# Flamingo gated block on one core: first loads and TensorE's first products in another order

## The reference, cut to what matters

```
x = x + tanh(g_xattn) * attention(layernorm(x), ctx, ctx, Wq, Wk, Wv)
x = x + tanh(g_ffn) * ffn(layernorm(x), ...)

attention: qh = q Wq^T, kh = k Wk^T, vh = v Wv^T
           scores = causal(qh kh^T / 16); probs = softmax(scores, over the queries)
           out = probs vh
ffn:       xq = quantised(x), gate and up = xq times quantised weights (256 to 704)
           h = quantised(silu(gate) * up); out = h times quantised w_down
```

## Time and profile before

| | |
|---|---|
| time, median of 3 runs | 107.29 us (106.71 to 107.92) |
| the profiled execution's own time | 106.97 us |
| its span | 105.2 us |
| PE / PEld busy | 97.9 us (93%) / 75.0 us (71%) |
| DVE / ACT / POOL busy | 80.6 / 66.1 / 43.4 us |

### The profile page before, as it was taken

How to read it: one execution, slowest core, us unless ns; L and a number is a source line. 1 busy time by engine, 2 the same in 40 slices (tenths; PEclk the granted TensorE clock), 3 DMA queues, 4 the chain that set the end, 5 groups by cost and what they waited for, 6 DMA issues and landing times.

```text
span 105.2 us, 1740 instructions
## 1 busy us (share of the span) xinstructions
PE 97.9 (93%) x564; PEld 75.0 (71%) x564; DVE 80.6 (77%) x211; ACT 66.1 (63%) x125; POOL 43.4 (41%) x78
## 2 busy tenths in 40 slices
PE   7999999999999999999989986999999697899990
PEld 2278888988989898887778973444444386889970
DVE  0544395497999979868597979559999998879991
ACT  0421071657980836639707978789888989799800
POOL 6030345056280835635606595045785560350000
DMA  2999999999305020020754800000000000004555
GB/s 43 329 378 319 393 421 423 411 408 407 119 2 48 0 49 4 18 39 3 148 101 100 161 13 0 0 6 3 0 0 0 0 0 0 0 6 184 215 199 199
DMA packets 11177, 13.54 MB, mean 129 GB/s; under 512 B 6433, under 2 KB 7713, under 8 KB 11169
## 3 DMA queue, kind: packets, MB, share of 16 engines
q1 hardware_dynamic: 10304, 12.39, 36.3%
q10 hardware_dynamic: 864, 1.05, 2.9%
HBM read 10.09 MB, written 2.10 MB: 116 GB/s over the span
## 4 chain that ended last, share of the span: by engine, by line
PE 43%; DVE 26%; DMA 13%; POOL 5%; issue 5%; ACT 4%; ACTq 1%; DVEq 0%; POOLq 0%
PE ps L459 10%; DVE hmax L1087 9%; PE ps L680 9%; PE ps L479 7%; DMA wvT<-in_wvT 5%; PE ps L497 5%; DMA r_wide<-spread 4%; DVE shared L1082 4%; DMA spread<-rstd 4%; PE ps L629 3%; POOL shared L430 2%; DVE bn L916 2%; DVE xs L910 2%; PE ps L685 2%; PE ps L509 2%
## 5 line engine op out<-in xcount | busy, mean ns | idle before, releaser
L629 PE MATMUL ps<-xq,wguT 128*128 128x512 bf16 x80 | 17.4, 379 | 0.8 <-DVE xq L1062 0.8
L430 POOL TENSOR_TENSOR shared<-up_sb,silu 128x1024 f32<-128x1024 f32 x5 | 11.8, 2365 | 9.5 <-ACT up_sb L826 9.5
L629 PEld LDWEIGHTS ps<-xq,wguT 128*128 128x128 bf16 x80 | 7.8, 97 | 10.2 <-issue 1.0
L459 PE MATMUL ps<-wvT,shared 128*128 128x256 f32 x56 | 13.3, 381 | 0.2 <-DMA wvT<-in_wvT 0.2
L479 PE MATMUL ps<-shared,a_sb 128*128 128x256 f32 x56 | 13.3, 380 | 0.0
L1087 DVE TENSOR_REDUCE hmax<-shared 128x1 f32<-128x2048 f32 (+1 forms) x6 | 12.6, 2108 | 0.6 <-POOL shared L430 0.2
L821 ACT ACTIVATE silu<-ps,gu_scale 128x1024 f32<-128x1024 f32 x10 | 11.1, 1113 | 2.3 <-PE ps L629 2.3
L497 PEld LDWEIGHTS ps<-uT,shared 128*128 128x128 f32 x64 | 10.7, 191 | 2.5 <-DVE uT L888 1.3
L497 PE MATMUL ps<-uT,shared 128*128 128x256 f32 (+1 forms) x64 | 12.0, 331 | 0.5 <-DVE uT L888 0.4
L459 PEld LDWEIGHTS ps<-wvT,shared 128*128 128x128 f32 x56 | 10.6, 190 | 2.0 <-DMA shared<-in_xc 0.6
L722 ACT ACTIVATE probs<-neg_scores,neg_max 128x256 f32<-128x256 f32 x8 | 4.1, 508 | 12.4 <-DVE neg_max L896 12.3
(11 more groups left out here) (120 smaller groups left out, 189.0 us busy)
## 6 DMA issues: line engine op xcount, KB each, us to landing
shared<-in_xc SPq DMA_DIRECT2D x6, 512.0 KB, 10.7
out<-xn SPq DMA_DIRECT2D x7, 256.0 KB, 2.0
xs<-in_x SPq DMA_DIRECT2D x3, 512.0 KB, 8.3
shared<-in_wgu SPq DMA_DIRECT2D x3, 512.0 KB, 7.7
wd<-in_wd SPq DMA_DIRECT2D x1, 896.0 KB, 11.7
shared<-in_xc SPq DMA_DIRECT2D x3, 256.0 KB, 6.4
xs<-in_x ACTq DMA_DIRECT2D x2, 256.0 KB, 5.5
r_wide<-spread SPq DMA_DIRECT2D x4, 128.0 KB, 4.5
```

Source lines behind the costliest of these rows:

```text
L430: nc.gpsimd.tensor_tensor(hid[:, 2 * i + 1, :], up_sb[i % 2][:], silu1[i % 2][:], ALU.mult).then_inc(hid_done[1], 1)
L459: last = nc.tensor.matmul(bank2(VB[b])[:, k, :], ctxT(b)[:, e, k * P:(k + 1) * P], weights[:, e, :], start=(e == 0), stop=(e == KT - 1))
L629: last = nc.tensor.matmul(bank(4 * half + 2 * g + c), wguT[:, i, g, k, :], xq[:, k, col:col + CH], start=(k == 0), stop=(k == KT - 1))
```

## The change

The order of the first transfers. Before, the SP queue carried half 0 of Wq, all of Wk, ctxT(0), half 0 of xT(0), xT(1), ctxT(1); the ACT queue half 1 of Wq, x of batch 0, Wv, half 1 of xT(0), x of batch 1, the scalars. After:

- SP: half 0 of Wq, half 0 of Wk, ctxT(0), half 0 of x of batch 0, half 0 of xT(0), ctxT(1), x of batch 1; then the wait ahead of the bulk is for half 1 of xT(0) in place of Wv;
- ACT: half 1 of Wq, half 1 of Wk, Wv, half 1 of x of batch 0, half 1 of xT(0), xT(1), the scalars.

Each half is 128 KB, each whole 256 KB. TensorE runs 9 warming products in place of 10, waits for each half of Wk by itself, does both value tiles of batch 0 ahead of the projection of batch 0, and the first value tile of batch 1 behind that projection. In the first pass of the loop `spread_deviation(1)` stands behind `project_queries(1)` and not ahead of it, and only the second value tile of batch 1 is left there. DVE does the statistics of batch 1 behind `scale_queries(0, ...)` in place of ahead of it.

```
--- before.py
+++ after.py
@@ -42,7 +42,7 @@
 MASKED = -1e30
 SCORE_SCALE = float(D) ** -0.5
 
-WARM_AT_START = 10
+WARM_AT_START = 9
 WARM_BEFORE_MAX = 2
 WARM_AT_BARRIER2 = 7
 FIRST_SLOTS = 6
@@ -191,7 +191,7 @@
 
 
         wq_here = [sem(f"wq_here{h}") for h in range(KT)]
-        wk_here = sem("wk_here")
+        wk_here = [sem(f"wk_here{h}") for h in range(KT)]
         wv_here = sem("wv_here")
         wv_g_ready = sem("wv_g_ready")
         scalars_here = sem("scalars_here")
@@ -304,12 +304,13 @@
                 sp.dma_start(wgu[:, 2 * n:2 * n + 2], wgu_in[:, 2 * n:2 * n + 2]).then_inc(wgu_here[n], 16)
 
             sp.dma_start(wq_sb[:, 0], wq_in[:, 0]).then_inc(wq_here[0], 16)
-            sp.dma_start(wk_sb[:], wk_in).then_inc(wk_here, 16)
+            sp.dma_start(wk_sb[:, 0], wk_in[:, 0]).then_inc(wk_here[0], 16)
             sp.dma_start(ctxT(0), xc_in[0, :, 0]).then_inc(c_here[0], 16)
+            sp.dma_start(xs[:, 0, :], x[:, 0, :]).then_inc(x_here[0], 16)
             sp.dma_start(xT(0)[:, 0], xc_in[0, :, 1, 0]).then_inc(xT0_here[0], 16)
-            sp.dma_start(xT(1), xc_in[1, :, 1]).then_inc(xT1_here, 16)
             sp.dma_start(ctxT(1), xc_in[1, :, 0]).then_inc(c_here[1], 16)
-            sp.wait_ge(wv_here, 16)
+            sp.dma_start(xs[:, QT:2 * QT, :], x[:, QT:2 * QT, :]).then_inc(x_here[1], 16)
+            sp.wait_ge(xT0_here[1], 16)
             load_x(2)
             load_xc(2)
             load_wgu(0)
@@ -526,8 +527,8 @@
 
 
             warm_up(WARM_AT_START, AT)
-            pe.wait_ge(wk_here, 16)
             for h in range(KT):
+                pe.wait_ge(wk_here[h], 16)
                 pe.wait_ge(wq_c_ready, h + 1)
                 for e, bk in enumerate((X2, AT)):
                     last = nc.tensor.matmul(bank(bk)[:, 0:D], wq_c[:, h, e * P:(e + 1) * P], wk_sb[:, h, :],
@@ -536,7 +537,9 @@
                         last.then_inc(a_mm, 1)
             pe.wait_ge(c_here[0], 16)
             pe.wait_ge(wv_here, 16)
-            values_tile(0, 0)
+            for k in range(QT):
+                last = values_tile(0, k)
+            last.then_inc(v_done, 1)
             for f in range(KT):
                 for e in range(KT):
                     pe.wait_ge(xT0_here[e], 16)
@@ -547,16 +550,15 @@
                 if f == 0:
                     pe.wait_ge(consts, 4)
                     spread_deviation(0)
-            values_tile(0, 1).then_inc(v_done, 1)
+            pe.wait_ge(c_here[1], 16)
+            values_tile(1, 0)
 
             for b in range(LAST - 1):
                 scores(b)
+                project_queries(b + 1)
                 if b == 0:
                     spread_deviation(1)
-                project_queries(b + 1)
-                if b == 0:
-                    pe.wait_ge(c_here[1], 16)
-                    values(1)
+                    values_tile(1, 1).then_inc(v_done, 1)
                 if b + 2 < LAST:
                     values(b + 2)
                 else:
@@ -706,10 +708,11 @@
         @block.scalar
         def _(act):
             act.dma_start(wq_sb[:, 1], wq_in[:, 1]).then_inc(wq_here[1], 16)
-            act.dma_start(xs[:, 0:QT, :], x[:, 0:QT, :]).then_inc(x_here[0], 16)
+            act.dma_start(wk_sb[:, 1], wk_in[:, 1]).then_inc(wk_here[1], 16)
             act.dma_start(wvT[:], wvT_in).then_inc(wv_here, 16)
+            act.dma_start(xs[:, 1, :], x[:, 1, :]).then_inc(x_here[0], 16)
             act.dma_start(xT(0)[:, 1], xc_in[0, :, 1, 1]).then_inc(xT0_here[1], 16)
-            act.dma_start(xs[:, QT:2 * QT, :], x[:, QT:2 * QT, :]).then_inc(x_here[1], 16)
+            act.dma_start(xT(1), xc_in[1, :, 1]).then_inc(xT1_here, 16)
             act.dma_start(scalars[:], scalars_in).then_inc(scalars_here, 16)
 
             def deviation_out(b):
@@ -859,7 +862,7 @@
         @block.vector
         def _(dve):
             def stats1(b):
-                dve.wait_ge(x_here[x_group(b)], 16)
+                dve.wait_ge(x_here[x_group(b)], 32 if b == 0 else 16)
                 for t in range(QT):
                     last = nc.vector.bn_stats(bn1[:, b, t, :], xs[:, QT * b + t, :])
                 last.then_inc(bn1_done, 1)
@@ -974,11 +977,12 @@
                     nc.vector.tensor_scalar(clip_diag[:, n, :], ident[:], clip_scale[:, n:n + 1], None,
                                             ALU.mult).then_inc(clip_diag_done, 1)
 
-            for b in range(2):
-                stats1(b)
-                variance1(b)
+            stats1(0)
+            variance1(0)
             for f in range(KT):
                 scale_queries(0, f)
+            stats1(1)
+            variance1(1)
             dve.wait_ge(consts, 3)
 
             for b in range(LAST - 1):
```

## The result

The changed kernel took 109.4 us (median of 6 runs, 108.06 to 109.97), the kernel before 107.3 (6 runs, 106.59 to 107.92) on the same chip. The ratio is 1.0152, with a 95% interval from 1.0099 to 1.0205. Each ratio in this document leaves out the runs that lie over 1.5% above the fastest of their kernel, here 3 of the 6, which is why it is smaller than 109.4 over 107.3. The profiled execution took 109.78 us with a span of 108.0 (before: 106.97 and 105.2): it is one of the three longest, and shows a loss of 2.8 us where the ratio means 1.6. Measured again on another chip, the ratio was 1.0086 (1.0050 to 1.0123): slower again, by less.

The account below looks back on a forecast made before the run. TensorE's own stream was taken as the bound up to 38 us; 0.60 us gained less a 0.13 us wait gives 0.47, so 106.97 profiled becomes 106.5, and 106.8 against the median of 107.29; range 106.1 to 107.7.

Parts of the forecast that it names:

- Queues and the bulk: Bulk loads behind the first transfers: start 0.65 us later, hidden by 1 us at DVE's first read; price without cover 0.65.
- the sum: Whole kernel: 0.60 us gained less 0.13 us of wait is 0.47 us, and nothing later takes it back.
- First values: TensorE's first value tiles, needing ctxT(0) and Wv: landing at 6.55 in place of 7.29, 0.8 us gained at their start.
- the transfers interleave, and the order does little: Rival on the first loads: Wv lands at 7.2 again, x is hidden, nothing gained, 107.3 to 107.4 us; chance 0.18.
- xT(0): Input of batch 0's projection: same 1536 KB ahead, lands at 7.94, hidden by 0.4 us behind both value tiles.
- The first deviation: Transposes of `spread_deviation(0)`: x of batch 0 lands at 7.2, `rstd1` stands at 9.3 to 9.4, TensorE waits 0.15 us.
- slower: the first deviation comes late: Rival at `spread_deviation(0)`: x lands at 7.94 or later, wait 0.9 us, loss 0.3 us, 107.6 us; chance 0.11.
- A: TensorE's first product after warming, on Wk, 8 slots (1.73 us): starts at 4.77 in place of 5.21, second half at 5.70.
- `scores(0)`: TensorE's scores of batch 0: start at 11.35, the 0.15 us of idle before them gone.
- `attend(0)`: TensorE's `attend(0)`: waits 0.13 us for `vh`, since ACT's exponentials wait for the moved `spread_deviation(1)`.
- Statistics of batch 1: On DVE, moved behind uT: 11.1 to 12.0, `rstd1` at 13.0, asked for at 14.4, so hidden.
- The clock: Rival at TensorE's start: the clock rises late, costing 0.15 us or 0.9 to 1.7, 107.9 us if usual; chance 0.06.

Follow-up runs that it names:

- b3: The kernel before with only the bulk's gate later: the bulk waits for context 1 in place of Wv; 109.7 us, ratio 1.0236.
- e1: b3 with batch 4 taken out of the transfers through DRAM, its deviation spread by two TensorE transposes; 106.58 us, ratio 1.0017 to the kernel before.
- a1: The changed kernel measured once more, with no edit; 107.44 us, ratio 1.0086 to the kernel before.
- a3: The changed kernel with the wait ahead of the bulk put back from xT(0) to Wv; 106.81 us, ratio 1.0022 to the kernel before.
- e2: The changed kernel with batch 4 taken out of the transfers through DRAM, its deviation spread by two TensorE transposes; 107.12 us, ratio 1.0059 to the kernel before.
- b4: a4 with ACT's copy of the second deviation moved behind the exponentials and values of batch 0; 107.36 us, ratio 1.0005 to the kernel before.
- a4: The kernel before with its own loads and only the new order on TensorE and DVE; 106.45 us, ratio 0.9996.
- d1: b3 with the four spread transfers issued on ACT's queue in place of SP's; 107.08 us, ratio 0.9966 to the kernel before.
- d2: The changed kernel with the four spread transfers issued on ACT's queue in place of SP's; 108.58 us, ratio 1.0147 to the kernel before.

## Why the prediction was wrong, point by point

It gave 106.8 us (106.1 to 107.7) and 0.07 to slower by over 1%; measured were 109.4 and 1.52%.

**The step that failed most** is in "Queues and the bulk": the bulk's start 0.65 us later was "hidden by 1 us; the next steps on it come later still", and with it the sentence of the sum that "nothing behind `attend(0)` takes it back". I priced the gate by the first reader of the first transfer. The cost came from the last thing behind the bulk, the spread of batch 4, for which no row had been read. The rows had the hint: the chain passes through `r_wide`, and in the same trace `scores(7)` waited 0.77 already, so this ring had no slack. By b3 against e1 a late gate costs up to 2.2% by this one link; in the changed kernel 1.49 of the 2.8 us of the profile stand behind the start of `scores(1)`, and by the ratios of a1 and a3 the gate is 0.64%. That the gate would be 0.65 us later was too small as well: xT(0)'s second half landed at 9.82, and the bulk went out at 9.88, against about 7.3 before. In other profiles of the changed kernel it landed at 8.3 to 9.1, which fits a1's smaller loss.

**First values**: forecast 6.55, measured 7.39, with Wv at about 7.3. The step "256 KB less ahead is 0.6 to 0.9 us less" failed: 1024 KB ahead landed when 1280 had. The formula of the Trainium skill (page "DMA: Bandwidth & Descriptors", section on the anatomy of one DMA) gave an estimate of 6.7, also too early. This wasn't the bad luck of one execution: in none of the 6 profiles with these loads did Wv land before 6.87. The rival "the transfers interleave, and the order does little" had 7.2 for this landing, the mean of the six; it was wrong in its result, since it took x as hidden.

**xT(0)** was to be hidden by 0.4 us. Its halves landed at 9.1 and 9.8 in place of 7.94, and TensorE waited 0.17 and 0.45 us for them. That cost nothing here, since the transposes behind it waited for the deviation in any case; it delayed the gate.

**The first deviation**: forecast an idle time of 0.15, measured 0.98 in this execution, 0.41 to 0.73 in others. x's second half landed at 8.94, not 7.2; the way from there to the transposes, forecast as 2.2, took 2.2. The rival "slower: the first deviation comes late" had the mechanism and its point of decision, 7.65, and I gave it 0.11. (The working gives this wait as 0.8 in one place and 0.9 in the rival, for the same landing at 7.94; 7.94 and 2.15 less 9.19 is 0.9.) It alone makes a loss of under 1%. With 0.47 us of forecast gain turned into 0.45 us of cost (e2 less e1), the head is mis-sized by 0.9 us.

**What held.** A starts at 4.84 (4.77) and its second half at 5.78 (5.70), waiting for `wq_c`, which was last either way: the halves of Wk landed at 4.1 and 4.3, earlier than the forecast 4.6 (whose own sum, 5.44 less 0.75, is 4.69). No idle time stands before `scores(0)`. `attend(0)` waits 0.16 (0.13) for `vh`; b4 took this away and gained nothing measurable. Statistics of batch 1 are hidden. The clock was no issue: it reads 1.00, and A's slots are 0.2 us. TensorE's new order has the ratio 0.9996 by itself (a4): its forecast benefit depended on landings, which never came.

## What to carry to other kernels

When a load is held back, don't ask only who reads it first: follow its queue to the last small transfer behind it, and ask whether that one's lateness can be made up. A write to memory that is read back, once per batch, forms a ring; if write, read and period are about equal, one late turn stays late to the end, so start such a ring when the large loads are through (e1), or keep the gate of the loads where it was (a3). And bytes ahead forecast a landing badly in the first 10 us: Wv landed at 7.2 in the mean with 256 KB less ahead of it, and at 7.3 without, and two profiles with the same loads differ by as much as such a forecast would win. Look at the times of all runs, too, before calling a kernel cured: d1's median hides two groups 2 us apart.

## What the runs showed of the hardware

A transfer of 1 KB took 2.6 to 3.4 us to landing with little in flight, and 5.7 us when a broadcast read of 4.4 us on its own queue had 4 us still to run (b3). A read on another engine's queue lengthened it in the same way (d2, 4.6 us with 3.2 to run). Issued 0.26 us ahead of such a read, it took 2.9 us (d1). The Trainium skill (page "DMA: Bandwidth & Descriptors", section "Queues, rings and completion order") says that the increment of the semaphore is an ordered write that lands only after all earlier writes of that DMA engine, across its queues. The runs agree with that in the relation of the durations; no run shows the mechanism itself.

With first loads of 128 KB in place of 256 KB, 1077 KB were moved between 2 and 6 us in the mean of 7 profiles, against 1187 in 13, on the same two queues; the ranges overlap.
